# Linear attention: GpSimd's first split behind the second norm, and the next layer's first weights and chunk prepared in the last batch

## The chip, the cores and the metric

The kernel runs on one core of a Trainium2 chip. A core has five engines with queues of their own: PE (TensorE, matmuls), DVE (VectorE), ACT (ScalarE), POOL (GpSimd) and SP (SyncE, which here only issues transfers). Engines wait for each other through semaphores. The metric is the device time of one execution in microseconds (us), the median of three runs.

## What is computed

Two transformer layers over 4 batches of 1024 tokens with 512 features. The change touches the second layer: a linear attention, and the feed-forward network behind it. The reference, cut to these:

```python
# linear attention (16 heads of 32; x is the normalized output of layer 0)
Q = jax.nn.relu(x @ Wq.T + bq); K = jax.nn.relu(x @ Wk.T + bk); V = x @ Wv.T + bv
Q = Q * decay; K = K * decay                       # exp(-pos / n)
KV = jnp.einsum('bhnd,bhne->bhde', K, V); Ksum = K.sum(axis=2)
Z = 1.0 / (jnp.einsum('bhnd,bhd->bhn', Q, Ksum)[..., None] + EPS)
out = jnp.einsum('bhnd,bhde->bhne', Q, KV) * Z
x = layernorm(x + out @ Wo.T + bo)
# feed-forward
X = x.reshape(-1, H).astype(jnp.float16)
D = gelu(X.astype(jnp.float32) @ W0.T + bias0).astype(jnp.float16)
E = D.astype(jnp.float32) @ W1.T + bias1
x = layernorm(x + E.astype(jnp.float16))
```

Wherever a product of 32-bit values has to keep its accuracy, both sides are split into a high part (rounded to the matmul's 32-bit format, "fp32r") and a low part (value minus high part), and the products of the parts are summed.

## The kernel before

The program is a row of phases; each allocates its buffers and semaphores, runs one block in which every engine has its own queue of instructions, and ends with a barrier of all engines. A semaphore that starts above zero is incremented by GpSimd at the start of its phase, in the order in which the code allocates them (line 63).

**Linear attention (`phase_linear_attention`, 503 us).** It works in chunks of 512 tokens, two a batch. Vector takes layer 0's output `y` in three passes (`quantize`, L1931 to L1935), adds the residual (`add_x1`, L1944) and normalizes (`LayerNorm`: four statistics L1206, aggregates L1210, on GpSimd an add and the power -0.5 in `pool_part`, L1193 and L1195, then on Vector four normalizing passes L1216). TensorE transposes the chunk (L1834); ScalarE copies the high part out of PSUM (L1798), Vector makes the low part (`part_lo`, L1951). TensorE then makes queries, keys and values (all matmuls of `partials` stand under L1164), four PSUM banks at a time. ScalarE finishes the queries (L1820), Vector adds the biases to keys (L1968) and values (L1974), GpSimd adds the output bias to the residual (L1772) and applies the decay (L1780, L1786). Then come the products of keys and values (taken by Vector at L1994), those with the queries (L1907), the division (L2011), transposes of the result, and the output projection, half by half, which Vector adds to the reloaded residual (L2024) and normalizes; SyncE stores each chunk to `x3_dram` (L1745). For batch b, Vector also prepares batch b+1. The work of all batches but the last stands in a hardware loop, that of the last behind it (`batches`).

The output weights `wo` are loaded into the buffer `ks`, which later holds the keys. ScalarE makes their high part and GpSimd their low part (`split_loader`, L99), two halves of 1024 columns. GpSimd does this between the first chunk's `pool_part` and the second's:

```python
ln_a.pool_part(pool, 0)
split_lo(pool)
ln_a.pool_part(pool, 1)
```

The phase ends when the last chunks are stored and landed and the first chunk of `x3` has been loaded for the next phase.

**Last layer (`phase_ffn1`, 498 us).** GpSimd builds a 16-bit identity (L2122, L2124). Vector casts chunk 0 to 16 bit (L2235), TensorE transposes it (L2179), ScalarE copies it to `xT` (L2152). Then, for each of 16 hidden tiles of each of 8 chunks: eight matmuls into a bank (`hidden`), gelu on ScalarE (L2165), a cast on GpSimd (L2141), eight matmuls into four output banks (`to_y`, L2205). TensorE is one hidden tile ahead. Both weights are loaded and split on Vector (L2242, L2244) from the start of the phase on, in 16 blocks of 1024 columns in turn; TensorE waits for the blocks in order.

## Time and profile before

| what | value |
|---|---|
| median of three runs | 2501.93 us (2501.62 to 2502.35) |
| the profiled execution's own time | 2500.06 us |
| its span | 2498.4 us |
| mean granted clock of TensorE | 0.983 of full |
| TensorE busy | 2377.2 us, 95% |
| VectorE, ScalarE, GpSimd busy | 1210.2, 817.8, 867.4 us |
| the chain that ended last | PE 19%, all other engines 0% |

The profile is of one execution. Its span runs from the first to the last instruction; its own time adds what lies around it. TensorE is busy nearly always, so a microsecond of another engine counts only where TensorE then waits. A busy TensorE need not be a fast one: its granted clock is 1.0 (2.4 GHz) or 0.5 (1.2 GHz).

### The profile page before, as it was taken

Reading aid. Unit: us, or ns where it says so; the run is one execution under the profiler, and the core shown is the slowest. Engines: PE = TensorE matmul, PEld = TensorE weight load, DVE = VectorE, ACT = ScalarE, POOL = GpSimd, SP = SyncE. Lnnn points to the kernel's source line nnn. Section 1 sums busy time; section 2 is a strip of 40 time slices with the busy share of each in tenths; the row PEclk is TensorE's granted clock in tenths of the full one; section 3 lists DMA queues with packets and bytes.
Section 4 is the critical chain, followed back from the end, with each engine's and each line's share of the span. In section 5 each row is a group of like instructions: output and inputs, shape, how many; then the busy total and the mean of one; then the engine's idle time right before and its main releaser. Section 6 shows DMA issues by size and latency. Waiting matters only on the chain. (4 is left out here: it accounts for less than half of the span.)

```text
span 2498.4 us, 39792 instructions
## 1 busy us (share of the span) xinstructions
PE 2377.2 (95%) x12757; PEld 1781.4 (71%) x12757; DVE 1210.2 (48%) x2540; ACT 817.8 (33%) x1387; POOL 867.4 (35%) x1097
## 2 busy tenths in 40 slices
PE   7999899999999999899999985999999799999997
PEld 5888655555555558688888874888888678888886
DVE  3334477777777758322222217676863551112211
ACT  3222255555555544344444431111111022222221
POOL 2000065565665642233333335242515022222221
PEclk9999999999999999999999997999999999999999
DMA  6885344545445337412121104040311250000100
GB/s 236 285 292 201 114 112 118 131 116 134 114 118 138 91 118 270 118 35 51 34 50 34 51 32 159 17 168 34 134 50 51 85 156 34 34 34 34 36 32 34
DMA packets 210065, 255.16 MB, mean 102 GB/s; under 512 B 68931, under 2 KB 106819, under 8 KB 209989
## 3 DMA queue, kind: packets, MB, share of 16 engines
q1 hardware_dynamic: 194084, 210.04, 28.5%
...
## 5 line engine op out<-in xcount | busy, mean ns | idle before, releaser
L177 DVE CUSTOM_DVE_ANT_0 junk<-psum,causal 128x896 bf16<-128x896 f32 (+7 forms) x512 | 373.6, 751 | 169.3 <-PE psum L887 145.0
L996 ACT ACTIVATE p_probs<-psum 128x512 f32<-128x512 f32 (+1 forms) x640 | 317.9, 555 | 274.9 <-PE psum L900 270.0
L1499 POOL TENSOR_TENSOR p_h_lo<-p_h,p_h_hi 128x512 fp32r<-128x512 f32 x128 | 164.3, 1284 | 307.9 <-ACT p_h_hi L1524 307.9
L900 PE MATMUL psum<-qst,kst 98*128 98x512 f32 (+3 forms) x768 | 223.6, 370 | 6.4 <-POOL p_ones L739 5.9
L2141 POOL CAST p_h<-p_h 128x512 fp32r<-128x512 f16 x128 | 92.0, 719 | 372.9 <-ACT p_h L2165 372.9
L789 POOL TENSOR_SCALAR_AFFINE_SELECT p_probs<-p_probs 128x128 f32<-128x128 f32 x512 | 141.5, 298 | 227.7 <-ACT p_probs L996 224.5
L900 PEld LDWEIGHTS psum<-qst,kst 98*128 98x128 f32 x768 | 132.3, 191 | 111.8 <-DVE rowmax L177 42.6
L887 PE MATMUL psum<-kst,qst 96*128 96x128 f32 (+3 forms) x720 | 208.1, 364 | 0.0
L1164 PE MATMUL psum<-p_xT,p_w_hi 128*128 128x512 f32 x512 | 203.2, 397 | 0.7 <-ACT p_xT L2152 0.7
L1553 PE MATMUL psum<-tern,p_h_hi 128*128 128x512 f32 x512 | 199.4, 390 | 2.0 <-POOL p_h_lo L1499 2.0
L1164 PE MATMUL psum<-p_xT,p_w_lo 128*128 128x512 f32 x512 | 200.2, 391 | 0.0
L2205 PE MATMUL psum<-p_w_hi,p_h 128*128 128x512 f32 x512 | 199.4, 389 | 0.3 <-POOL p_h L2141 0.3
L1553 PE MATMUL psum<-tern,p_h_lo 128*128 128x512 f32 x512 | 199.2, 389 | 0.0
L2205 PE MATMUL psum<-p_w_lo,p_h 128*128 128x512 f32 x512 | 199.2, 389 | 0.0
L2165 ACT ACTIVATE p_h<-psum,p_b 128x512 f16<-128x512 f32 x128 | 88.0, 687 | 330.6 <-PE psum L1164 330.6
L1516 ACT ACTIVATE p_h<-psum,ffn_b,alpha 128x512 f32<-128x512 f32 x128 | 99.8, 780 | 260.3 <-PE psum L1164 260.3
L887 PEld LDWEIGHTS psum<-kst,qst 96*128 96x128 f32 x720 | 125.3, 191 | 67.8 <-DVE rowmax L177 41.1
L2254 DVE TENSOR_TENSOR p_e<-psum,p_b 128x512 f16<-128x512 f32 x32 | 19.9, 682 | 299.9 <-PE psum L2205 299.9
L916 PE MATMUL psum<-p_probs,v 128*32 128x512 f32 (+3 forms) x1536 | 157.9, 498 | 1.8 <-ACT p_probs L996 1.1
L927 PE MATMUL psum<-p_probs,p_ones 128*32 128x512 f32 (+3 forms) x1536 | 154.8, 490 | 0.0
L403 PE MATMUL psum<-p_xT_hi,p_w_hi 128*128 128x512 f32 x256 | 100.8, 394 | 17.5 <-DVE p_w_lo L99 17.5
L1553 PEld LDWEIGHTS psum<-tern,p_h_hi 128*128 128x128 f32 x512 | 96.1, 188 | 22.7 <-POOL p_h_lo L1499 1.5
...
## 6 DMA issues: line engine op xcount, KB each, us to landing
...
```

Of the source, the lines that this page charges most:

```text
L177: return dve.tensor_tensor_reduce(view(junk[:, 0:n]), bank, view(self.causal[:, SEQ - n:SEQ]), 1.0, FLOOR, ALU.add, ALU.max, self.rowmax[: ...
L403: mm = pe.matmul(bank, lhsT, rhs, start=(n == 0), stop=(n == 3 * KT - 1))
L789: pool.affine_select(out=blk, in_=blk, compare_op=ALU.is_ge, fill=0.0, base=0, pattern=[[1, P]], channel_multiplier=-1).then_inc(p_masked, 1)
L887: mm = pe.matmul(psum[:, bank, 0:keys], qst[slot][0:KD, c, g, tile * P:(tile + 1) * P], kst[slot][0:KD, g, k0:k0 + keys], start=True, stop ...
L900: mm = pe.matmul(psum[:, bank, col:col + CH - q0], kst[s][0:KD + 2, g, j * P:(j + 1) * P], qst[s][0:KD + 2, c, g, q0:CH], start=True, stop ...
L916: mm = pe.matmul(O_BANK[g * HD:(g + 1) * HD, q0:CH], vs[s][:, j, g * HD:(g + 1) * HD], probs[:, n % 2, g, col:col + CH - q0], start=(n == ...
L927: mm = pe.matmul(SUM_BANK[g * HD:(g + 1) * HD, q0:CH], ones[:, :], probs[:, n % 2, g, col:col + CH - q0], start=(n == half_at), stop=(n + ...
L996: act.activation(probs[:, n % 2, g, col:CH], psum[:, banks_of(s, "s", st)[0], col:CH], ACT.Exp, scale=SM_SCALE).then_inc(p_ready, 1)
L1164: mm = pe.matmul(bank, lhsT, rhs, start=(n == 0), stop=(n == len(terms) - 1))
L1499: pool.tensor_tensor(h_lo[:, m % 2, :], h[:, m % 2, :], f32(h_hi[:, m % 2, :]), ALU.subtract).then_inc(hl_done, 1)
L1553: mm = pe.matmul(Y.bank(m), src[:, t % 2, tok], tern2[:, t, :], start=(t == 0 and part == 0), stop=(t == HT - 1 and part == 1))
L2205: mm = pe.matmul(Y.bank(m), h[:, t % 2, a * P:(a + 1) * P], w[:, t, :], start=(t == 0 and part == 0), stop=(t == HT - 1 and part == 1))
```

## The change

1. GpSimd does both chunks' `pool_part` first, waits for the second norm (`ln_a.normed`), and only then splits `wo`. Vector waits for this split before it writes its first keys, and no longer before its loop. The semaphores `y_loaded` and `x1_loaded` are allocated first in the phase.
2. In the last batch SyncE loads, as buffers come free, the four row tiles of `W0` (2048 columns each), the first four of the 16 tiles of `W1`, chunks 0 and 1 of `x3`, and the bias. ScalarE makes the five high parts behind the last queries, Vector the low parts in three groups: two between keys and values of the second half, one behind the values, two behind the low parts of the output. The order is tile 3 of `W0`, then `W1`'s, then tiles 0, 1, 2. The buffers are those of weights, `y` and residual that are then free.
3. In the last batch Vector casts chunk 0 to 16 bit; TensorE transposes it between the two halves of the output projection, ScalarE copies it to `xT` and loads the gelu table; behind the output projection TensorE makes hidden tile 0 of the last layer. GpSimd builds the identity at the start of the linear attention.
4. In the last batch each statistic follows its add. SyncE no longer waits at the end of the phase for the stores of `x3`; SyncE and Vector wait for them in the last layer, before they use them.
5. The last layer starts with hidden tile 1, and splits only the twelve other tiles of `W1`. The PSUM banks of hidden tiles, transposes and outputs are 0 and 1, 2 and 3, 4 to 7.

The diff, cut to its core:

```diff
@@ -1202,8 +1202,15 @@
     def find_statistics(self, dve, n, src):
 
         for t in range(CT):
-            dve.wait_ge(self.summed, self.FROM + n * CT + t + 1)
-            dve.bn_stats(self.stats[:, t, :], src(t)).then_inc(self.got_stats, 1)
+            self.statistics_of(dve, n, t, src)
+        self.aggregate(dve, n)
+
+    def statistics_of(self, dve, n, t, src):
+        dve.wait_ge(self.summed, self.FROM + n * CT + t + 1)
+        dve.bn_stats(self.stats[:, t, :], src(t)).then_inc(self.got_stats, 1)
+
+    def aggregate(self, dve, n):
+
...
@@ class LastLayer @@
+    FIRST = 4
+
+    def hidden(self, pe, bank, c, t):
+        return partials(pe, bank, [(w[k][:, t * P:(t + 1) * P], self.xT[:, c, k, :]) for k in range(KT) for w in (self.w0_hi, self.w0_lo)])
...
+        y_loaded = [sem("p5_y_loaded0", 16), sem("p5_y_loaded1")]
+        x1_loaded = sem("p5_x1_loaded", 16)
         wo_hi = sb("p5_wo_hi", [P, KT, D], F32R)
...
-        y_loaded = [sem("p5_y_loaded0", 16), sem("p5_y_loaded1")]
-        x1_loaded = sem("p5_x1_loaded", 16)
...
+        parts = [(after.w0_raw[k], after.w0_hi[k], after.w0_lo[k]) for k in (3, 0, 1, 2)]
+        parts.insert(1, (after.w1_raw, after.w1_hi, after.w1_lo))
...
@@ -1727,26 +1773,48 @@
                 sp.wait_ge(ln_a.summed, ln_a.FROM + CT)
                 load_x1(sp, 0, 1)
 
+                def load_tile(n, k):
+                    sp.dma_start(after.w0_raw[k], after.w0[k * P:(k + 1) * P, :]).then_inc(raw_loaded[n], 16)
+
+                def load_next(b):
+
+                    sp.wait_ge(ln_a.summed, ln_a.FROM + 8 * b + 8)
+                    load_tile(0, 3)
+                    for c in range(2):
+                        sp.wait_ge(x3_stored[c], 1 + 16)
+                        sp.dma_start(by_tile(after.x3[c]), tiles(x3_dram[c])).then_inc(next_loaded, 16)
+                    sp.dma_start(after.b0c, after.b0).then_inc(b0_loaded, 16)
+
+                def load_weights(b):
+
+                    for c in range(2):
+                        sp.wait_ge(residual_stored[c], 16 * b + 16)
+                    sp.wait_ge(t_lo, 1 + 16 * b + 8)
+                    sp.dma_start(after.w1_raw, after.w1[0:after.FIRST * P, :].rearrange("(t p) n -> p t n", p=P)).then_inc(raw_loaded[1], 16)
+                    for k, freed in enumerate((q_relu, k_biased, v_done)):
+                        sp.wait_ge(freed, 8 * b + 8)
+                        load_tile(2 + k, k)
+
                 def body(b, last):
+                    if last:
+                        load_next(b)
                     for c in range(2):
                         sp.wait_ge(x2_biased, 2 * b + c + 1)
                         sp.dma_start(tiles(residual[2 * b + c]), chunk(x2, c)).then_inc(residual_stored[c], 16)
+                    if last:
+                        load_weights(b)
                     for c in range(2):
                         sp.wait_ge(residual_stored[c], 16 * b + 16)
                         sp.sem_inc(passed, 1)
                         sp.wait_ge(t_lo, 1 + 16 * b + 8 + 4 * c + 4)
                         sp.sem_inc(passed, 1)
                         sp.dma_start(chunk(ks, c), tiles(residual[2 * b + c])).then_inc(residual_loaded[c], 16)
-                    if last:
-                        sp.wait_ge(x3_stored[0], 1 + 16 * b)
-                        sp.dma_start(by_tile(next_x3[:, :]), tiles(x3_dram[0])).then_inc(next_loaded, 16)
                     for c in range(2):
                         sp.wait_ge(ln_b.normed, 8 * b + 4 * c + 4)
                         sp.dma_start(tiles(x3_dram[2 * b + c]), chunk(ks, c)).then_inc(x3_stored[c], 16)
                 batches(sp, body)
-                for c in range(2):
-                    sp.wait_ge(x3_stored[c], 1 + 16 * BATCH)
-                sp.wait_ge(next_loaded, 16)
+                sp.wait_ge(next_loaded, 32)
+                sp.wait_ge(b0_loaded, 16)
...
+                build(11, pool.memset(ident16[:, :], 0.0))
+                build(12, pool.affine_select(out=ident16[:, :], in_=ident16[:, :], compare_op=ALU.not_equal, fill=1.0, base=0,
+                                             pattern=[[-1, P]], channel_multiplier=1))
                 ln_a.setup(pool)
                 ln_b.setup(pool)
-                ln_a.pool_part(pool, 0)
+                for c in range(2):
+                    ln_a.pool_part(pool, c)
+                pool.wait_ge(ln_a.normed, 2 * CT)
                 split_lo(pool)
-                ln_a.pool_part(pool, 1)
...
@@ -1808,6 +1880,12 @@
                         for c in range(2):
                             load_y(act, b + 1, c)
                         load_x1(act, b + 1, 0)
+                    def next_hi():
+                        for n in range(KT + 1):
+                            act.wait_ge(raw_loaded[n], 16)
+                            raw, hi, _ = [flat(part) for part in parts[n]]
+                            act.activation(hi, raw, ACT.Copy).then_inc(raw_hi, 1)
+
                     for c in range(2):
                         if c == 1:
                             part_hi(b, 1, a_x)
@@ -1818,10 +1896,17 @@
                             m = b_q(c, g)
                             B.wait_full(act, b, m)
                             act.activation(qT[:, g, c * CH:(c + 1) * CH], B.bank(m), ACT.Relu, bias=bq_c[:, g:g + 1]).then_inc(q_relu, 1)
+                    if last:
+                        next_hi()
                     for c in range(2):
                         part_hi(b, c, a_oT)
                     if not last:
                         part_hi(b + 1, 0, a_x)
+                    else:
+                        for k in range(KT):
+                            A.wait_full(act, b + 1, k)
+                            act.activation(aT_hi[:, 0, k, :], A.bank(k).bitcast(F16)[:, 0:CH], ACT.Copy).then_inc(x_ready, 1)
+                        act.preload_act_table(ACT.Gelu)
...
@@ -1918,6 +2003,18 @@
                             B.fill(partials(pe, B.bank(m), product(c, 3, tok(t), everything, True)), m)
                         if c == 0 and not last:
                             x2_transposes(b + 1, 0)
+                        if c == 0 and last:
+                            pe.wait_ge(built, 12)
+                            pe.wait_ge(x_cast, 1)
+                            for k in range(KT):
+                                free_a(b + 1, k)
+                                for t in range(CT):
+                                    mm = pe.transpose(A.bank(k).bitcast(F16)[:, tok(t)], x16[:, t, tok(k)], ident16[:, :])
+                                A.fill(mm, k)
+                    if last:
+                        pe.wait_ge(x_ready, KT)
+                        pe.wait_ge(raw_lo, KT + 1)
+                        after.hidden(pe, psum[:, 0, :], 0, 0)
...
                 def body(b, last):
                     def keys(c):
+                        if c == 0:
+                            dve.wait_ge(w_done, n_w)
                         dve.wait_ge(x3_stored[c], 1 + 16 * b)
                         for t in range(CT):
                             B.wait_full(dve, b, b_k(c, t))
@@ -1974,6 +2072,12 @@
                             dve.tensor_tensor(vs[:, CT * c + t, :, 0:P], heads(B.bank(b_v(c, t))), heads(bias[:, 1, :]), ALU.add).then_inc(v_done, 1)
 
 
+                    def next_lo(first, to):
+                        for n in range(first, to):
+                            dve.wait_ge(raw_hi, n + 1)
+                            raw, hi, lo = [flat(part) for part in parts[n]]
+                            dve.tensor_tensor(lo, raw, f32(hi), ALU.subtract).then_inc(raw_lo, 1)
+
                     if not last:
                         quantize(b + 1, 0)
                     part_lo(b, 1, a_x, 0)
@@ -1981,7 +2085,14 @@
                         keys(c)
                         if not last:
                             add_x1(b + 1, c)
+                        if last and c == 1:
+                            next_lo(0, 2)
                         values(c)
+                        if last and c == 1:
+                            next_lo(2, 3)
+                            dve.wait_ge(next_loaded, 32)
+                            dve.wait_ge(q_done, 8 * b + 8)
+                            dve.tensor_copy(flat(x16), after.x3[0]).then_inc(x_cast, 1)
                         if not last:
                             ln_a.find_statistics(dve, 2 * b + 2 + c, x2_tile(c))
                         if c == 0 and not last:
@@ -2013,17 +2124,24 @@
                             ins.then_inc(o_done, 1)
                     for c in range(2):
                         part_lo(b, c, a_oT, 8)
+                    if last:
+                        next_lo(3, 5)
                     if not last:
                         ln_a.normalize_tiles(dve, 2 * b + 3, x2_tile(1), x2_tile(1))
                     for c in range(2):
                         dve.wait_ge(residual_loaded[c], 16 * b + 16)
+                        x3_tile = lambda t: ks[:, CT * c + t, :]
                         for t in range(CT):
                             m = b_out(CT * c + t)
-                            at = ks[:, CT * c + t, :]
                             B.wait_full(dve, b, m)
-                            dve.tensor_tensor(at, B.bank(m), at, ALU.add).then_inc(ln_b.summed, 1)
-                        x3_tile = lambda t: ks[:, CT * c + t, :]
-                        ln_b.vector_part(dve, 2 * b + c, x3_tile, x3_tile)
+                            dve.tensor_tensor(x3_tile(t), B.bank(m), x3_tile(t), ALU.add).then_inc(ln_b.summed, 1)
+                            if last:
+                                ln_b.statistics_of(dve, 2 * b + c, t, x3_tile)
+                        if last:
+                            ln_b.aggregate(dve, 2 * b + c)
+                        else:
+                            ln_b.find_statistics(dve, 2 * b + c, x3_tile)
+                        ln_b.normalize_tiles(dve, 2 * b + c, x3_tile, x3_tile)
 ...
@@ phase_ffn1 @@
+        H = Banks(nc, ctx, "p6_hbank", psum, 0, 2, 2 * HT, before=1)
+        h_done, h_used = sem("p6_h_done", 2), sem("p6_h_used", 1)
+        Y = Banks(nc, ctx, "p6_ybank", psum, 4, CT, 2 * CT)
+
+        T = Banks(nc, ctx, "p6_tbank", psum, 2, 2, 2 * KT)
+        bias_loaded = sem("p6_bias_loaded")
+        x_loaded = [sem(f"p6_x_loaded{c}", 16) for c in range(2)]
...
                sp.dma_start(b1r[:, :], rows(b1)).then_inc(bias_loaded, 16)
-                load_x(0, 1)
+                for c in range(2):
+                    sp.wait_ge(got.x3_stored[c], 1 + 16 * BATCH)
```

**How the order of instructions changes.** GpSimd, start of the linear attention, behind its memsets (`p_wo_lo` is the low part of `wo`, `p_k` and `ffn_rows` the buffer `ks`; x2 means two in a row). Before:

```order
L1186 MEMSET p_ln_a_power 128x4
L1186 MEMSET p_ln_b_power 128x4
L1193 TENSOR_SCALAR p_ln_a_vareps<-p_ln_a_meanvar 128x4
L1195 TENSOR_TENSOR p_ln_a_rstd<-p_ln_a_vareps,p_ln_a_power 128x4
L99 TENSOR_TENSOR p_wo_lo<-p_k,p_wo_hi 128x1024 x2
L1193 TENSOR_SCALAR p_ln_a_vareps<-p_ln_a_meanvar 128x4
L1195 TENSOR_TENSOR p_ln_a_rstd<-p_ln_a_vareps,p_ln_a_power 128x4
L106 UNCONDITIONAL_BRANCH
L106 ISA
L1772 TENSOR_TENSOR p_x<-p_x,p_bias 128x2048
```

With the change:

```order
L1829 MEMSET ident 128x128
L1830 AFFINE_SELECT ident<-ident 128x128
L1186 MEMSET p_ln_a_power 128x4
L1186 MEMSET p_ln_b_power 128x4
L1193 TENSOR_SCALAR p_ln_a_vareps<-p_ln_a_meanvar 128x4
L1195 TENSOR_TENSOR p_ln_a_rstd<-p_ln_a_vareps,p_ln_a_power 128x4
L1193 TENSOR_SCALAR p_ln_a_vareps<-p_ln_a_meanvar 128x4
L1195 TENSOR_TENSOR p_ln_a_rstd<-p_ln_a_vareps,p_ln_a_power 128x4
L99 TENSOR_TENSOR p_wo_lo<-ffn_rows,p_wo_hi 128x1024 x2
L106 UNCONDITIONAL_BRANCH
L106 ISA
L1844 TENSOR_TENSOR la_x<-la_x,p_bias 128x2048
```

The second root has moved ahead of the split, and the identity has been added ahead of both norms.

Vector, last batch, keys and values (`ffn_w_first` is the part of `W1`, `la_w_lo` takes tiles of `W0`, `p_decay_row` then holds the 16-bit chunk). With the change:

```order
L2048 TENSOR_TENSOR p_aT_lo<-psum,ffn_xT 128x512 x4
L2066 TENSOR_TENSOR ffn_rows<-psum,p_bias 128x512 x4
L2072 TENSOR_TENSOR p_v<-psum,p_bias 128x4x128 x4
L2066 TENSOR_TENSOR ffn_rows<-psum,p_bias 128x512 x4
L2079 TENSOR_TENSOR ffn_w_3<-la_y,ffn_w_3 128x2048
L2079 TENSOR_TENSOR ffn_w_first<-la_x,ffn_w_first 128x2048
L2072 TENSOR_TENSOR p_v<-psum,p_bias 128x4x128 x4
L2079 TENSOR_TENSOR la_w_lo<-ffn_w_raw,la_w_hi 128x2048
L2095 CAST p_decay_row<-ffn_x 128x2048
L2105 TENSOR_TENSOR p_kv<-psum,p_same_head 128x128
L2106 TENSOR_SCALAR p_kv<-p_same_head,psum 128x4
```

The rows with 128x2048 are new: two subtractions ahead of the second half's values, one subtraction and the cast behind them; two more stand behind the low parts of the output.

TensorE, end of the linear attention and start of the last layer. Before:

```order
L1164 MATMUL psum<-p_wo_lo,p_aT_hi 128x512
L1716 UNCONDITIONAL_BRANCH
L2170 UNCONDITIONAL_BRANCH
L2179 MATMUL psum<-p_ident,p_x 128x128 x16
L1164 MATMUL psum<-p_xT,p_w_hi 128x512
L1164 MATMUL psum<-p_xT,p_w_lo 128x512
L1164 MATMUL psum<-p_xT,p_w_hi 128x512
L1164 MATMUL psum<-p_xT,p_w_lo 128x512
```

With the change:

```order
L1164 MATMUL psum<-p_wo_hi,p_aT_lo 128x512
L1164 MATMUL psum<-p_wo_lo,ffn_xT 128x512
L1164 MATMUL psum<-ffn_xT,la_w_hi 128x512
L1164 MATMUL psum<-ffn_xT,la_w_lo 128x512
L1164 MATMUL psum<-ffn_xT,la_w_hi 128x512
L1164 MATMUL psum<-ffn_xT,la_w_lo 128x512
L1164 MATMUL psum<-ffn_xT,la_w_hi 128x512
L1164 MATMUL psum<-ffn_xT,la_w_lo 128x512
L1164 MATMUL psum<-ffn_xT,ffn_w_3 128x512 x2
L1762 UNCONDITIONAL_BRANCH
L2257 UNCONDITIONAL_BRANCH
L106 UNCONDITIONAL_BRANCH
```

The 16 transposes have moved ahead of the second half of the output projection, and the eight matmuls of hidden tile 0 ahead of the phase's end.

## Rows read from the trace of the kernel before

**Rows 1.** Waits of TensorE over the whole span: us in total, times, longest.

```profile
PE psum L1834 <- DVE p_x L1216: 28.3, 2, 15.7
PE psum L2179 <- POOL p_ident L2124: 15.9, 1, 15.9
```

**Rows 2.** Timeline, linear attention, chunk 1: start, us, engine, line, operation.

```profile
1517.03 1.27 DVE L1931 TENSOR_SCALAR la_y<-la_y,la_quant 128x2048 f32<-128x2048 f32 x1
1517.30 6.59 POOL L99 TENSOR_TENSOR p_wo_lo<-p_k,p_wo_hi 128x1024 fp32r<-128x1024 f32 x2 [6.97 <-ACT p_wo_hi L94]
1518.34 3.31 DVE L1933 TENSOR_SCALAR la_y<-la_y 128x2048 f32<-128x2048 f32 x1
...
1525.01 2.50 DVE L1944 TENSOR_TENSOR p_x<-la_y,la_x 128x512 f32<-128x512 f32 x4
1527.70 0.94 ACTq L1711 DMA_DIRECT2D la_y<-ffn_out  x2
1531.94 4.49 POOL L1772 TENSOR_TENSOR p_x<-p_x,p_bias 128x2048 f32<-128x2048 f32 x1
1532.00 8.92 DVE L1216 TENSOR_SCALAR p_x<-p_x,p_ln_a_meanvar,p_ln_a_rstd 128x512 f32<-128x512 f32 x4 [1.58 <-POOL p_ln_a_rstd L1195]
1541.06 3.67 PE L1834 MATMUL psum<-ident,p_x 128*128 128x128 f32 x16 [12.61 <-DVE p_x L1216]
...
1550.78 0.69 DVE L1968 TENSOR_TENSOR p_k<-psum,p_bias 128x512 f32<-128x512 f32 x1 [2.03 <-PE psum L1164]
...
DMA to landing us min/median/max: 5.7/6.7/7.8
```

**Rows 3.** Timeline, start of the linear attention.

```profile
1499.49 1.29 DVE L1931 TENSOR_SCALAR la_y<-la_y,la_quant 128x2048 f32<-128x2048 f32 x1 [2.16 <-POOLq L63]
1499.87 1.05 POOL L1756 MEMSET p_same_head<- 128x132 f32 x1 [10.27 <-issue]
...
1503.39 2.50 DVE L1944 TENSOR_TENSOR p_x<-la_y,la_x 128x512 f32<-128x512 f32 x4
```

**Rows 4.** Timeline, end of the linear attention and start of the last layer.

```profile
1983.94 11.26 SPq L1745 DMA_DIRECT2D x<-p_k  x2
1988.29 2.46 DVE L1206 BATCH_NORM_STATS2 p_ln_b_stats<-p_k 128x6 f32<-128x512 f32 x4
1992.87 1.92 DVE L1216 TENSOR_SCALAR p_k<-p_k,p_ln_b_meanvar,p_ln_b_rstd 128x512 f32<-128x512 f32 x4 [1.58 <-POOL p_ln_b_rstd L1195]
...
2003.55 1.04 PE L2179 MATMUL psum<-p_ident,p_x 128*128 128x128 f16 x8 [15.90 <-POOL p_ident L2124]
...
2012.46 0.49 PE L2205 MATMUL psum<-p_w_hi,p_h 128*128 128x512 f32 x1 [0.30 <-POOL p_h L2141]
```

**Rows 5.** Stretches: us, TensorE busy (instructions), granted clock, DMA share, GB/s.

```profile
1026.00:1027.00 1.00, 1.00 (x4) 0.53 0.67 116
...
1544.00:1546.00 2.00, 2.00 (x8) 0.56 0.00 0
```

**Rows 6.** Groups by line and form, and the timeline of the last batch.

```profile
L1320 ACT ACTIVATE p_o_hi<-pieces 128x2048 fp32r<-128x2048 f32 x3 | 5.8, 1919 | 15.2 <-PE psum L1164 11.8 <-PE psum L1344 3.4
L1372 DVE TENSOR_TENSOR p_o_lo<-pieces,p_o_hi 128x2048 fp32r<-128x2048 f32 x3 | 6.8, 2258 | 0.0
...
1945.26 0.29 DVE L1994 TENSOR_TENSOR p_kv<-psum,p_same_head 128x128 f32<-128x128 f32 x1 [2.16 <-PE psum L1164]
...
1961.81 1.09 ACT L1798 ACTIVATE p_aT_hi<-psum 128x512 fp32r<-128x512 f32 x2 [40.47 <-PE psum L1834]
...
1970.71 1.35 DVE L2024 TENSOR_TENSOR p_k<-psum,p_k 128x512 f32<-128x512 f32 x2 [3.18 <-DMA p_k<-residual]
```

**Rows 7.** Timeline, start of layer 0's feed-forward phase.

```profile
1020.10 0.39 SPq L1286 DMA_DIRECT2D x<-p_x  x1
...
1022.66 0.79 PE L1164 MATMUL psum<-ffn_xT_hi,tern 128*128 128x512 f32 x1 [5.59 <-POOLq L63]
```

153 lines of the change are left out of this document (75 added, 78 removed).

## Prediction, made before the change was measured

> **What bounds the kernel now.** The waits of TensorE come first, because TensorE is busy for 95% of the span: only its idle time can be taken away, or its work. Two of the waits lie in the phases that the change touches: 28.3 us in two waits for the first norm's output of the linear attention's first two chunks, and 15.9 us for the 16-bit identity at the start of the last layer [rows 1]. I then read the timelines around both places, engine by engine, for the chain that ends each wait, and last the clock.
>
> *Place A, start of the linear attention.* TensorE has chunk 0's queries, is through at 1528.45 and waits 12.61 us, until 1541.06 [rows 2]. Vector makes that wait: three quantizing passes over chunk 1 last from 1517.03 to 1525.01, 7.98 us, where the same three over chunk 0 last 3.90 (1499.49 to 1503.39) [rows 2, 3]. Add, statistics and the reciprocal root lead to 1532.00, and the four normalizing passes then take 8.92 us, where four such passes alone take 1.92 [rows 2, 4]. Both slow stretches lie beside GpSimd work: the split of the output weights (6.59 us) and the bias add (4.49 us) [rows 2].
>
> *Place B, end of the linear attention and start of the last layer.* The last statistics start at 1988.29, SyncE has issued the last store at 1995.20, and the first output matmul of the last layer is at 2012.46. Between them lie the store's landing, the barrier, the identity, 16 transposes and two hidden tiles, the first of them at half clock [rows 4].
>
> **The change, part by part.**
>
> *1. Start values.* GpSimd increments 21 semaphores when the phase begins. The one that Vector's first pass waits for was the 17th and is now the first. GpSimd's own first instruction starts 0.38 us after Vector's, with four increments between: 0.095 us each [rows 3]. Sixteen fewer would be 1.5 us; nothing is the other end, if the barrier is what lasts. I take 1.0, nearer to the increments, since Vector's wait ends on GpSimd's queue by the row itself. The added 16-bit memset and select lie between 1499.87 and the first root, which can't be asked for before four adds (2.50) and four statistics are through; with a memset at 1.05 they fit, and cost nothing [rows 3, 4].
>
> *2. GpSimd's split behind the second norm.* Vector's chunk 1 then runs without GpSimd's big operations: 7.98 becomes 3.90 and 8.92 becomes 1.92, together 11.08 us. With part 1 the norm ends 12.08 us earlier, and the transposes start at 1528.98. TensorE's own queue ends 1.0 earlier too, at 1527.45, so 12.61 us of idling become 1.5. In the kernel before the clock stood at its lower level (0.5, 1.2 GHz) from 1541.06 until about 1545.76 [rows 2, 5]; 4.7 us at half speed are 2.35 us of work lost. An idle time of 1.5 us is far shorter than the one after which it was low, so I give back all of that. **Place A gives 14.4 us.**
>
> What is late next is GpSimd: its split and first bias add, and what Vector does beside them. The next values' bank needs key tile 0, one projection (four banks of 2.72) after the key projection starts: 1528.98 + 1.84 (16 transposes, half of the 3.67 that they take at the low clock) + 10.88 = 1541.7. Vector has by then to quantize batch 1's first chunk beside GpSimd (7.98, as chunk 1 before), make four low parts and one key tile, all five 512 wide from PSUM at the key tile's 0.69: 1528.84 + 7.98 + 3.45 = 1540.3 [rows 2]. The slack is 1.4 us, and it depends on who goes first. In the rows, a single-input Vector pass that starts at 1518.34 lasts 3.31 instead of about 1.25: it starts while GpSimd's operation runs and ends 1.1 after that one must be through, so the two take turns by whole instructions.
>
> The Trainium skill, "SBUF — State Buffer", section on the two sides of SBUF, says the same in general: the pair of ports that VectorE and GpSimd share is an exclusive lock, held by whoever starts first for the whole instruction. By that rule GpSimd first means that Vector's third pass waits for the bias add as a whole, and the sum loses the 3.0 us of rival 2; by a shared bandwidth it would lose nothing. The trace agrees with the lock.
>
> *3. Weights in the last batch.* Five tiles of 2048 columns are loaded, copied on ScalarE (1.92 each) and subtracted on Vector (2.26 each) [rows 6]. ScalarE: the last load starts when the last value tile is biased (1943.1, that is 1945.26 less its idle 2.16), lands 5.7 to 7.8 later [rows 2, 6], and is copied by 1952.8 at the latest; ScalarE is next needed at 1961.81. Slack 9.0. Vector, behind the keys: two subtractions, 4.5 us, delay two or three value tiles, not the last, since TensorE makes one per 2.72. Behind the values: one subtraction and the 16-bit cast (at most 1.3, as a single-input pass), 3.6 us from 1943.1, so the first of the four key-value products is taken 1.4 late, and each later one comes as it did. Behind the low parts, from 1967.53 (1970.71 less 3.18): two subtractions until 1972.05, so the first residual add is 1.3 us late; add and statistics take 1.3 of every 2.72, and the delay is gone by the fourth tile. Cover gone in each case: up to 1.4. SyncE's queue now holds 3 MB ahead of the residual store; only two loads wait for that store, that of the second weights and, much later in the program, the residual's own, and both have room. All of it: zero.
>
> *4. The transition.* TensorE gets 16 transposes of 16 bit between the two halves of the output projection. Eight of them take 1.04 us at the low clock [rows 4], so 16 take 1.05 to 1.7 (as 32-bit ones); I take 1.3. The last chunk's chain starts that much later: 1989.59 for its first statistic. Three of four statistics now lie between the adds (2.46 / 4 each, 1.85 off): the last store is issued by 1989.59 + 6.91 - 1.85 = 1994.65. Its landing is no longer waited for. At the other phase start where TensorE had its operands ready, it began 2.17 us after the last store was issued (1020.49 to 1022.66), behind 14 increments [rows 7]; now it needs four of them. Ends 1.0 and 2.17, taken 1.3: hidden tile 1 starts at 1995.95. Hidden tile 0 has been made before the barrier, and its gelu and cast run beside tile 1. The clock: TensorE idles about 5 us, and in two rows it took 4.2 and 4.7 us of matmuls until the clock was up again [rows 2, 5, 7]; I take low from the start for 4.5 us, 2.25 lost (ends: never low, 0; 6.4 us as at 2003.55, 3.2). Hidden tile 1 is 8 matmuls, 1.81 at full clock (2.72 / 12 each). At full speed the first output matmul would thus stand at 1995.95 + 1.81 + 2.25 = 2000.0, against 2012.46. **Place B gives 12.45 us.** The twelve tiles of the second weights that are still split after the barrier are needed only from the fifth step on.
>
> *Sum.* 14.4 + 12.45 = 26.85. The profiled execution took 2500.06, so 2473.2; the median of the runs shown is 1.87 above that execution, so **2475.1**. Everything after place A and place B is TensorE without waits, so both shifts last to the end.
>
> **The rivals.**
> 1. *My sum, within its bounds:* from 2472.3 (clock never low, 0.5 more at place A) to 2478.4. Chance 0.5.
> 2. *GpSimd gets the ports first at place A.* Then its two halves of the split (4.49 / 2 = 2.25 each) and the bias add alternate with Vector's passes (1.1 each): 1531.2, 1532.3, 1534.55, 1535.65, 1540.1, 1541.2; low parts and key tile end at 1544.65, and TensorE waits 3.0 us. It decides by batch 1's first y: issued at 1522.6, 5.7 to 7.8 until landing, 1528.3 or later, against 1528.84 when Vector is free [rows 2]. Time 2478.1. For: 0.5 us of margin. Against: the first of two loads is the quicker. Chance 0.23.
> 3. *The last batch or the transition does only a part.* Either the phase's end still waits for the store (what lies between 1995.20 and 2003.55, less 2.17: up to 6.2; 2479 to 2481), or the delays of part 3 reach TensorE, each up to 1.4 and more if a load is late. Time 2479 to 2485. Chance 0.24.
> 4. *Slower than before.* ScalarE takes the five weight tiles in order ahead of the copies of the attention's transposed output. If the last load is late by more than 9.0 us, each further microsecond holds TensorE; slower than before from 36 us late on (9.0 + 26.85), 2502 and more. No load in the rows takes over 7.8. Chance 0.01; 0.02 remain for no difference.
>
> **How the numbers follow.** A run of this kernel can be told from another one by about 0.2%, 5 us; all cases but the last two are faster by more. The predicted time is that of case 1. The range takes in case 1, case 2 with its own late end (2481), and most of case 3: 2470.5 to 2484. Faster 0.97, same 0.02, slower 0.01.
>
> **What would show it.** TensorE's wait for the norm in one piece of about 15 us and one under 2; Vector's chunk 1 passes at 1.3 us, its normalizing at 1.92; the split of the output weights beside batch 1's quantizing; no more than 1 us of waiting before the first values (3 would be rival 2). At the end: 16 transposes between the output halves; a gap of about 5 us from hidden tile 0 to tile 1; tile 1 at half clock. Wrong would be: a wait of TensorE for low parts, keys or weights in the last batch, a gap over 8 us at the transition, or steps of the last layer longer than before.

## The result, and the profile after

The changed kernel takes 2477.77 us (median of 4 runs, 2477.44 to 2478.64). The kernel before, timed on the same chip in the same sitting, takes 2502.14 us (4 runs, 2501.62 to 2502.47). The ratio is 0.9903, with a 95% interval of 0.9886 to 0.9920: faster, by 24.4 us. The forecast was 2475.1, with a range of 2470.5 to 2484.

The page of the changed kernel, parts of its head and its busy times:

```profile
span 2475.2 us, 39666 instructions
PE 2376.8 (96%) x12757; PEld 1779.9 (72%) x12757; DVE 1197.2 (48%) x2525; ACT 827.1 (33%) x1392; POOL 867.7 (35%) x1097
```

TensorE's busy time is what it was (2377.2 before); the span is shorter by 23.2 us, and 22.8 us of that are idle time of TensorE (121.2 us before, 98.4 now). Its mean granted clock went from 0.983 to 0.987. The waits of TensorE (total, times, longest) that answer to [rows 1]:

```profile
PE psum L1919 <- DVE la_x L1223: 16.3, 2, 14.8
PE psum L1164 <- POOLq L63: 11.4, 2, 5.8
PE psum L1164 <- DVE p_v L2072: 4.4, 4, 1.5
```

The wait for the norm's output has gone from 28.3 us in two pieces to 16.3, of which 14.8 is the first chunk's. The 15.9 us for the 16-bit identity are gone. In their place the second line, which was 5.6 us in one piece, has a second piece of 5.8 us: the gap at the barrier. The wait for the values, 2.9 us before, has grown to 4.4, by one piece of 1.5: that one is new, and the forecast did not have it.

**Place A.** Start of the linear attention, timeline of the changed kernel: start, duration, engine, line, operation, instructions, idle time before it. It answers to [rows 2, 3]. (All of this execution is already 0.30 us later than the one before when the phase begins.)

```profile
1498.75 1.29 DVE L2028 TENSOR_SCALAR la_y<-la_y,la_quant 128x2048 f32<-128x2048 f32 x1 [1.12 <-POOLq L63]
1516.67 1.28 DVE L2028 TENSOR_SCALAR la_y<-la_y,la_quant 128x2048 f32<-128x2048 f32 x1
1527.56 1.92 DVE L1223 TENSOR_SCALAR la_x<-la_x,p_ln_a_meanvar,p_ln_a_rstd 128x512 f32<-128x512 f32 x4 [1.58 <-POOL p_ln_a_rstd L1195]
1529.39 1.28 DVE L2028 TENSOR_SCALAR la_y<-la_y,la_quant 128x2048 f32<-128x2048 f32 x1
1529.56 6.70 POOL L99 TENSOR_TENSOR p_wo_lo<-ffn_rows,p_wo_hi 128x1024 fp32r<-128x1024 f32 x2 [2.03 <-DVE la_x L1223]
1529.61 1.97 PE L1919 MATMUL psum<-ident,la_x 128*128 128x128 f32 x16 [1.53 <-DVE la_x L1223]
1530.71 3.30 DVE L2030 TENSOR_SCALAR la_y<-la_y 128x2048 f32<-128x2048 f32 x1
1536.22 5.62 POOL L1844 TENSOR_TENSOR la_x<-la_x,p_bias 128x2048 f32<-128x2048 f32 x1
1542.33 0.41 SPq L1803 DMA_DIRECT2D residual<-la_x  x1
1546.77 7.33 DVE L2041 TENSOR_TENSOR la_x<-la_y,la_x 128x512 f32<-128x512 f32 x4 [3.54 <-DMA residual<-la_x]
1546.81 5.13 POOL L1844 TENSOR_TENSOR la_x<-la_x,p_bias 128x2048 f32<-128x2048 f32 x1
1554.03 2.47 DVE L2072 TENSOR_TENSOR p_v<-psum,p_bias 128x512 f32<-128x512 f32 x4
1554.85 0.47 PE L1164 MATMUL psum<-ffn_xT,la_w_hi 128*128 128x512 f32 x1 [1.48 <-DVE p_v L2072]
1557.86 0.69 ACT L1898 ACTIVATE p_qT<-psum,p_bq 128x512 f32<-128x512 f32 x1 [25.50 <-PE psum L1164]
1560.58 0.69 ACT L1898 ACTIVATE p_qT<-psum,p_bq 128x512 f32<-128x512 f32 x1 [2.03 <-PE psum L1164]
```

The first pass starts 1.12 us after what came ahead, not 2.16. Chunk 1's first pass takes 1.28 and the normalizing 1.92, as alone. The transposes run at once, and in 1.97 us instead of 3.67. Behind them GpSimd's split (6.70 us) lies beside batch 1's quantizing, whose second and third passes take 3.30 and 3.29. New is what follows: four residual adds take 7.33 us, not 2.50, beside GpSimd's second bias add; the first value is copied only at 1554.03, and TensorE waits.

**The last batch.** Timeline of the weight work that was moved there:

```profile
1920.19 2.28 DVE L2079 TENSOR_TENSOR ffn_w<-la_y,ffn_w 128x2048 fp32r<-128x2048 f32 x1
1920.48 5.98 POOL L1858 TENSOR_SCALAR ffn_rows<-ffn_rows,p_decay_col 128x512 f32<-128x512 f32 x1 [0.72 <-DVE ffn_rows L2066]
1922.39 2.29 DVE L2079 TENSOR_TENSOR ffn_w_first<-la_x,ffn_w_first 128x2048 fp32r<-128x2048 f32 x1
```

Each subtraction takes 2.25 to 2.3 us, as forecast from [rows 6]. Beside two of them one of GpSimd's key decays takes 5.98 us; the three ahead of it take 2.00. No wait of TensorE came of any of it.

**Place B.** The transition to the last layer, timeline, answering to [rows 4]:

```profile
1977.50 0.69 DVE L1210 BATCH_NORM_STATS2 p_ln_b_stats<-ffn_rows 128x6 f32<-128x512 f32 x1
1982.26 0.38 SPq L1814 DMA_DIRECT2D x<-ffn_rows  x1
1984.36 0.79 PE L1164 MATMUL psum<-ffn_xT,la_w_hi 128*128 128x512 f32 x1 [5.81 <-POOLq L63]
1984.36 0.69 ACT L2252 ACTIVATE p_h<-psum,ffn_b 128x512 f16<-128x512 f32 x1 [15.87 <-POOLq L63]
1992.76 0.69 ACT L2252 ACTIVATE p_h<-psum,ffn_b 128x512 f16<-128x512 f32 x1 [3.82 <-PE psum L1164]
```

Windows of the same stretch (us, busy time of TensorE, its weight loads, VectorE, ScalarE and GpSimd, then granted clock, share of the DMA engines, GB/s):

```profile
1982.00:1983.00 1.00, 0.00 (x0) 0.00 (x0) 0.24 (x1) 0.00 (x0) 0.00 (x0) 0.99 0.00 0
1983.00:1984.00 1.00, 0.00 (x0) 0.00 (x0) 0.00 (x0) 0.00 (x0) 0.00 (x0) 0.50 0.81 309
1989.00:1990.00 1.00, 1.00 (x4) 0.76 (x4) 0.83 (x2) 0.00 (x0) 0.73 (x1) 0.60 1.06 397
```

SyncE's last store is issued at 1982.26 and TensorE goes on at 1984.36; hidden tile 1 and more run at half clock until about 1989.7. For the accounts below, the same two anchors in the kernel before, the first query tile of chunk 1 and the third gelu of the last layer:

```profile
1569.82 0.69 ACT L1820 ACTIVATE p_qT<-psum,p_bq 128x512 f32<-128x512 f32 x1 [24.46 <-PE psum L1164]
2016.49 0.69 ACT L2165 ACTIVATE p_h<-psum,p_b 128x512 f16<-128x512 f32 x1 [3.53 <-PE psum L1164]
```

### The profile page after: what moved, and what is told of

It reads as the page before. It is cut to its first block and busy times, and to the rows that moved or that the text cites. A ratio compares the mean times of both kernels' runs of the same rounds, so it can differ in the third digit from the quotient of the medians.

```text
span 2475.2 us, 39666 instructions
## 1 busy us (share of the span) xinstructions
PE 2376.8 (96%) x12757; PEld 1779.9 (72%) x12757; DVE 1197.2 (48%) x2525; ACT 827.1 (33%) x1392; POOL 867.7 (35%) x1097
## 5 line engine op out<-in xcount | busy, mean ns | idle before, releaser
L1164 PE MATMUL psum<-ffn_xT,la_w_hi 128*128 128x512 f32 x512 | 202.9, 396 | 8.8 <-POOLq L63 5.8
L2252 ACT ACTIVATE p_h<-psum,ffn_b 128x512 f16<-128x512 f32 x128 | 88.0, 688 | 346.6 <-PE psum L1164 330.7
L1164 PE MATMUL psum<-ffn_xT,la_w_lo 128*128 128x512 f32 x512 | 200.5, 392 | 0.0
L2336 DVE TENSOR_TENSOR ffn_rows<-psum,p_b 128x512 f16<-128x512 f32 x32 | 19.9, 684 | 315.7 <-PE psum L2286 315.7
L2286 PE MATMUL psum<-p_w_hi,p_h 128*128 128x512 f32 x384 | 149.7, 390 | 0.0
L2286 PE MATMUL psum<-p_w_lo,p_h 128*128 128x512 f32 x384 | 149.5, 389 | 0.0
L1164 PEld LDWEIGHTS psum<-ffn_xT,la_w_hi 128*128 128x128 f32 x512 | 96.6, 189 | 29.3 <-POOLq L63 6.2
```

Of the source, the lines that this page charges most:

```text
L1164: mm = pe.matmul(bank, lhsT, rhs, start=(n == 0), stop=(n == len(terms) - 1))
L2286: mm = pe.matmul(Y.bank(m), h[:, t % 2, a * P:(a + 1) * P], w(t), start=(t == 0 and part == 0), stop=(t == HT - 1 and part == 1))
```

## The experiments

The kernel before was timed again beside each group of runs; its medians were 2501.02, 2501.71 and 2502.07 us, and 2502.14 above. So medians of different groups can differ by about 1 us for nothing. Where an effect is smaller, the timeline within the run decides, and the text says which of the two it goes by.

### Is it GpSimd's place that made chunk 1 slow?

Run *split_between* puts the split back between the two roots. With it goes GpSimd's wait for the second norm (`ln_a.normed`), which in the changed kernel keeps the bias add and the query decay off that norm as well:

```diff
-for c in range(2):
-    ln_a.pool_part(pool, c)
-pool.wait_ge(ln_a.normed, 2 * CT)
-split_lo(pool)
+ln_a.pool_part(pool, 0)
+split_lo(pool)
+ln_a.pool_part(pool, 1)
```

> The changed kernel with one part undone: GpSimd's split of the output weights stands between its two first reciprocal roots again; everything else stays. Theory (Vector's chunk 1 was slow because GpSimd's big operations lay beside it): the three quantizing passes take about 8 us again in place of 3.8, the norm behind them about 8.9 in place of 1.92, TensorE waits over 12 us before chunk 1's transposes and comes out of it at its lower clock, and the 1.48 us wait before the first values is gone. That is 12 to 13 us back: 2489.5 to 2491. Rival (chunk 1 was slow from its own load or from the late start): the passes stay near 1.3 us and the time within 2 us of 2477.8.

Measured: 2487.92 us (2487.53 to 2489.06), 10.2 more than the changed kernel; ratio to before 0.9948 (0.9931 to 0.9964), against 0.9903, which is 11.2 us.

```profile
1517.42 3.30 DVE L2029 TENSOR_SCALAR la_y<-la_y 128x2048 f32<-128x2048 f32 x1
1531.08 8.92 DVE L1223 TENSOR_SCALAR la_x<-la_x,p_ln_a_meanvar,p_ln_a_rstd 128x512 f32<-128x512 f32 x4 [1.58 <-POOL p_ln_a_rstd L1195]
1540.13 3.67 PE L1918 MATMUL psum<-ident,la_x 128*128 128x128 f32 x16 [12.64 <-DVE la_x L1223]
```

The second pass takes 3.30 us again (so does the third), the norm's four passes take 8.92, and TensorE waits 12.6 us for them. The slow passes lie beside the split and cost 4.08 us; the slow norm lies beside the bias add (from 1531.02, 4.49 us) and the query decay behind it, and costs 7.00. The run undoes both at once, so it shows that GpSimd's order made the 11 us; how they divide is read from the timeline, and no run has the one without the other. The wait before the first values is gone (2.9 us in all). The first query tile of chunk 1 stands at 1569.43, 11.57 later than in the changed kernel, and this run began the phase 0.45 earlier: 12.0 us, as the theory says. The medians lie 1.6 under the lower end of my range. 0.7 of that is the clock at the transition, which came back sooner in this run (first to third gelu 7.67 us, against 8.40); the rest is no more than groups of runs differ by.

*start_alone* is the kernel before with place A's parts alone (the order above; the three load semaphores allocated first; Vector's wait for the split of the output weights moved down):

```diff
+y_loaded = [sem("p5_y_loaded0", 16), sem("p5_y_loaded1")]
+x1_loaded = sem("p5_x1_loaded", 16)
...
-dve.wait_ge(w_done, n_w)
...
 def keys(c):
+    if c == 0:
+        dve.wait_ge(w_done, n_w)
```

> The kernel before with only the parts at the start of the linear attention: the split behind the second root, the three load semaphores ahead of the others, Vector's wait for the weights' load behind the quantizing passes. Nothing in the last batch or the transition. Theory (the two places add up, nothing is shared): the whole of place A and nothing of place B, 12 us off, 2489.5 to 2490.5, with Vector's passes as in the changed kernel. Rival (part of place B's gain comes from place A, or the other way round): outside 2488 to 2492.

Measured: 2489.64 us (2489.22 to 2491.28), 11.4 less than before in the same group; ratio 0.9956 (0.9939 to 0.9972). The first query tile of chunk 1 stands at 1558.06 there, against 1569.82 in the kernel before and 1557.86 in the changed one. This run began the phase 0.23 us later than the changed kernel, so place A is worth the same with and without place B, 12.3 us at that point. By the medians it is 11.4, and 11.9 more for all else in the changed kernel (their sum of 23.3 misses 24.4 by the 1.1 by which the kernel before differs between the two groups). Place B alone was not run.

### Part 1: the start values

*semaphores_late* allocates `y_loaded` and `x1_loaded` of the changed kernel behind the 16 others again.

> The changed kernel with the load semaphores of the first pass back behind 16 others, so GpSimd increments their start values last. Theory (Vector's first pass waits for that increment): the first pass starts 1.0 us later after the phase before, and the time is 1.0 us more, 2478.8. Rival (the barrier or another engine lasts longer): no change, 2477.8.

Measured: 2477.67 us (2477.11 to 2477.94), by the median no change. The timeline of this run:

```profile
1499.80 1.29 DVE L2028 TENSOR_SCALAR la_y<-la_y,la_quant 128x2048 f32<-128x2048 f32 x1 [2.31 <-POOLq L63]
1558.97 0.69 ACT L1898 ACTIVATE p_qT<-psum,p_bq 128x512 f32<-128x512 f32 x1 [25.19 <-PE psum L1164]
```

Vector's first pass does wait 2.31 us in place of 1.12, and the first query tile comes 1.11 us later (1558.97 against 1557.86), though this run began the phase 0.14 us earlier. So the increments are what Vector waited for, and the move is worth 1.2 us there. At the other end of the program only 0.6 are left (span 2475.8 against 2475.2): at the transition this run's clock came back 0.5 us earlier after hidden tile 1 (first to third gelu 7.86 us, against 8.40). The theory holds for the place; end to end, it is inside what these runs can tell.

### The new wait: adds beside a bias add

Vector's four adds, one by one, in the changed kernel (first and second):

```profile
1546.77 0.69 DVE L2041 TENSOR_TENSOR la_x<-la_y,la_x 128x512 f32<-128x512 f32 x1 [3.54 <-DMA residual<-la_x]
1547.38 5.11 DVE L2041 TENSOR_TENSOR la_x<-la_y,la_x 128x512 f32<-128x512 f32 x1
```

The second lasts 5.11 us: it ends 0.55 us after GpSimd's bias add does (1546.81 + 5.13 = 1551.94). Two runs ask whether that is the cause. *no_second_bias* leaves GpSimd's second bias add out but for 8 columns:

```diff
-pool.tensor_tensor(part, part, bias..., ALU.add).then_inc(x2_biased, 1)
+if c == 0:
+    pool.tensor_tensor(part, part, bias..., ALU.add).then_inc(x2_biased, 1)
+else:
+    pool.tensor_tensor(part[:, 0:1, 0:8], part[:, 0:1, 0:8], bias[:, 2:3, 0:8], ALU.add).then_inc(x2_biased, 1)
```

> The changed kernel without most of GpSimd's second output-bias add of each batch (the output bias is missing from the second half of each batch, but for 8 columns). It asks what makes the new wait of 1.48 us before the first values, where Vector's four residual adds take 7.33 us and start beside GpSimd's second bias add of 5.13 us. Theory (Vector and GpSimd lock each other out of SBUF's shared ports): the adds take 2.5 us, TensorE's wait before the first values is gone, the time 1.5 us less, 2476.3, and a little more in the eight batches if something there was hidden. Rival (the residual's store and load make the chunk late): the wait stays at 1.0 us or more, 2477.3 or above.

Measured: 2476.34 us (2474.70 to 2477.35).

```profile
1546.73 2.92 DVE L2044 TENSOR_TENSOR la_x<-la_y,la_x 128x512 f32<-128x512 f32 x4 [3.57 <-DMA residual<-la_x]
1558.78 0.69 ACT L1901 ACTIVATE p_qT<-psum,p_bq 128x512 f32<-128x512 f32 x1 [2.03 <-PE psum L1164]
```

*values_first* keeps all the work and puts the first chunk's adds behind its values:

```diff
 keys(c)
-if not last:
+if not last and c == 1:
     add_x1(b + 1, c)
...
 values(c)
+if not last and c == 0:
+    add_x1(b + 1, c)
```

> The changed kernel with the residual add of each batch's first chunk behind that batch's first values instead of ahead of them. Theory (TensorE's wait of 1.48 us before the first values comes from the 7.33 us adds that stand ahead of the values in Vector's queue): the values' first copy starts as soon as TensorE has made the tile, the wait is gone, the first query tile is 1.5 us earlier, 2476.3. Rival (the adds were free there and now delay the low parts or a later norm): the wait is gone and another of 1 us or more stands at the next chunk's transposes, 2477.5 to 2480.

Measured: 2476.26 us (2474.81 to 2476.93).

```profile
1553.77 1.99 POOL L1858 TENSOR_SCALAR ffn_rows<-ffn_rows,p_decay_col 128x512 f32<-128x512 f32 x1
1554.36 2.49 DVE L2041 TENSOR_TENSOR la_x<-la_y,la_x 128x512 f32<-128x512 f32 x4
1555.74 2.89 POOL L1858 TENSOR_SCALAR ffn_rows<-ffn_rows,p_decay_col 128x512 f32<-128x512 f32 x1
1559.19 0.69 ACT L1898 ACTIVATE p_qT<-psum,p_bq 128x512 f32<-128x512 f32 x1 [1.13 <-PE psum L1164]
```

The adds take 2.9 and 2.5 us, and TensorE's waits for values are back at 2.9 us in all. In *values_first* ScalarE takes the first query tile late, since the issue of a load that waits for the adds stands ahead in its queue, so the second one is the anchor: 1560.58 in the changed kernel, 1558.78 without the bias add, 1559.19 with the values first (in a run 0.34 us later at chunk 1's norm), that is 1.8 and 1.7 us earlier. With *no_second_bias* the adds start when they did (1546.73), after the same wait for the residual's store, and TensorE waits for nothing more than in the kernel before; so that store alone does not make TensorE wait, and the rival falls. The store has a part in it all the same. Vector was through with its keys at 1543.2 and waited 3.54 us for it, and only therefore did the adds start beside the second bias add, which began at 1546.81. No other wait of TensorE grew in *values_first*, so its rival falls too. The medians are 1.4 and 1.5 us lower, in the direction and size of the theory, but within what groups of runs can differ; the lengths of the adds carry the verdict.

### Place B, piece by piece

*store_waited* lets SyncE wait for the last stores again at the end of the linear attention:

```diff
+for c in range(2):
+    sp.wait_ge(x3_stored[c], 1 + 16 * BATCH)
 sp.wait_ge(next_loaded, 32)
```

> The changed kernel with the wait for the last output stores at the end of the linear attention put back. Theory (the transition is shorter by the store's landing): the barrier opens 4 to 6 us later, TensorE's gap between hidden tiles 0 and 1 grows from 5.8 to 10 to 12 us, 2482 to 2484. Rival (the stores land while the last statistics are made, and the gain is in the early tile alone): the gap stays under 7 us, and the time within 1 us of 2477.8.

Measured: 2482.40 us (2481.66 to 2483.01).

```profile
1984.07 0.38 SPq L1814 DMA_DIRECT2D x<-ffn_rows  x1
1990.04 0.79 PE L1164 MATMUL psum<-ffn_xT,la_w_hi 128*128 128x512 f32 x1 [9.69 <-POOLq L63]
```

From the last store's issue to TensorE's next matmul it is 5.97 us here, and 2.10 in the changed kernel: 3.9 us is what the landing costs, 4.6 with the clock and the rest by the medians.

*tile_behind* makes hidden tile 0 in the last layer, behind the barrier:

```diff
 pe.wait_ge(raw_lo, KT + 1)
-after.hidden(pe, psum[:, 0, :], 0, 0)
...
-H = Banks(nc, ctx, "p6_hbank", psum, 0, 2, 2 * HT, before=1)
+H = Banks(nc, ctx, "p6_hbank", psum, 0, 2, 2 * HT)
...
+H.fill(got.hidden(pe, H.bank(0), 0, 0), 0)
```

> The changed kernel with hidden tile 0 of the last layer made behind the barrier, as the kernel before does, instead of ahead of it; transposes and the rest stay early. Theory (the tile's 8 matmuls fill waiting time ahead of the barrier, and behind it they are on the path at the lower clock): hidden tile 0 costs 3.6 us there, minus nothing, since the clock's fall lasts for 5 us either way; TensorE's gap is 1.8 us longer on its front side. 1.8 us of work more on the path, and the clock's loss unchanged: 2479.5 to 2481.5. Rival (TensorE would otherwise wait for the gelu and its cast before the first output matmul, so the tile's time is hidden behind them): under 1 us.

Measured: 2481.18 us (2481.09 to 2481.87), 3.4 more.

```profile
1983.48 0.38 SPq L1814 DMA_DIRECT2D x<-ffn_rows  x1
1986.66 0.77 PE L1164 MATMUL psum<-ffn_xT,la_w_hi 128*128 128x512 f32 x1 [8.71 <-POOLq L63]
```

The last store's issue to the first matmul is 3.18 us, against 2.10: TensorE waits 1.1 us longer behind the barrier, by the row for GpSimd's queue at the line of the start values. The code gives a reason: this run's hidden tile 0 first waits for the two banks of the transposes, whose start values come 14 increments behind the one that hidden tile 1 waits for. In *semaphores_late* 16 increments took 1.19 us, and at that rate 14 take 1.0. No run moves them here, so this is worked out and not shown. With the tile's 1.8 us that makes 2.9, which is also by how much the third gelu is later (1996.89, less 1.21 by which this run's last statistics are later, against 1992.76). I had the 1.8 and not the 1.1. The early tile is worth 3 us.

*statistics_together* puts the last batch's statistics behind all four adds of their chunk:

```diff
-if last:
-    ln_b.statistics_of(dve, 2 * b + c, t, x3_tile)
...
+ln_b.find_statistics(dve, 2 * b + c, x3_tile)
```

> The changed kernel with the last batch's statistics behind all four residual adds of a chunk again, as in the kernel before. Theory (they stand on the chain from the last output matmul to the barrier): last store and barrier 1.85 us later, 2479.6. Rival (TensorE's last products pace the adds, so the statistics between them cost what they save, or SyncE's queue is later anyway): under 0.5 us.

Measured: 2478.92 us (2478.15 to 2480.24), 1.2 more.

```profile
1986.66 0.79 PE L1164 MATMUL psum<-ffn_xT,la_w_hi 128*128 128x512 f32 x1 [7.42 <-POOLq L63]
```

The gap grows by 1.61 us, three of four statistics as forecast (1.85) less a little; 0.3 of it comes back as clock.

### The clock, at both places

*filler_end* keeps TensorE at work ahead of the barrier, with 16 matmuls into a bank that nobody reads:

```diff
 after.hidden(pe, psum[:, 0, :], 0, 0)
+for _ in range(2):
+    after.hidden(pe, psum[:, 1, :], 0, 0)
```

> The changed kernel with two more copies of the first hidden tile's 8 matmuls behind it, into a bank that nothing reads: 3.6 us of unused work in TensorE's gap of 5.8 us. Theory (hidden tile 1 runs at 1.2 GHz because of the gap ahead of it, and the gap is free time): the granted clock stays at 1.0 through the transition, the first gelus of the last layer are 3.7 us apart from the start in place of 3.9 and 4.5, and the time is 1.8 to 2.5 us less, 2475.3 to 2476. Rival (the fall comes from what remains of the gap, or the filler's end itself holds the barrier): the clock falls as before or the gap grows, 2477.5 to 2480.

Measured: 2475.65 us (2475.53 to 2476.40), 2.1 less.

```profile
1984.61 0.49 PE L1164 MATMUL psum<-ffn_xT,la_w_hi 128*128 128x512 f32 x1 [2.13 <-POOLq L63]
1987.34 0.95 PE L2288 MATMUL psum<-ffn_w_first,p_h 128*128 128x512 f32 x3 [0.63 <-POOL p_h L2234]
1991.36 0.69 ACT L2254 ACTIVATE p_h<-psum,ffn_b 128x512 f16<-128x512 f32 x1 [3.84 <-PE psum L1164]
```

```profile
1983.00:1984.00 1.00, 0.00 (x0) 0.00 (x0) 0.00 (x0) 0.00 (x0) 0.00 (x0) 1.00 0.53 203
```

The clock stays at 1.00 through the gap, now 2.13 us long, and the matmul behind it takes 0.49 us in place of 0.79. From the first to the third gelu it is 6.71 us, not 8.40: 1.7 us. It isn't more because TensorE, no longer slow, now waits 0.63 us for GpSimd's cast ahead of the first output matmul. This is the term of 2.25 to 2.7 us of my sum, tested by itself.

*filler_start* does the same ahead of the first norm of the linear attention, with 40 matmuls of 128x512:

```diff
+for n in range(10):
+    partials(pe, psum[:, 4 + n % 4, :], [(w_hi[n % 3][:, k, 0:P], w_hi[n % 3][:, k, :]) for k in range(KT)])
 x2_transposes(0, 0)
```

> The changed kernel with 40 unused matmuls of 128x512 ahead of chunk 0's transposes, in TensorE's wait of 14.8 us for the first norm at the start of the linear attention. Theory (the wait leaves TensorE at 1.2 GHz, its 16 transposes take 3.67 us in place of 1.97 and the low parts behind them come later): the granted clock is 1.0 when the norm is through, the transposes take 2 us, and the first query tile comes 1.7 to 2.0 us earlier, 2475.8 to 2476.1. Rival A (the transposes are paced by something else): the first query tile comes less than 0.5 us earlier. Rival B (chunk 1's norm is the later one, so what chunk 0 gains TensorE waits before chunk 1): TensorE's wait of 1.53 us before chunk 1's transposes grows by what chunk 0 gained, 2477.5.

Measured: 2476.13 us (2476.03 to 2476.53), 1.6 less by the median.

```profile
1498.28 10.88 PE L1164 MATMUL psum<-la_w_hi 128*128 128x512 f32 x40 [1.64 <-PEq L68]
1511.44 3.34 PE L1919 MATMUL psum<-ident,la_x 128*128 128x128 f32 x16 [2.27 <-DVE la_x L1223]
```

```profile
1511.00:1512.00 1.00, 0.56 (x4) 0.56 (x5) 0.39 (x1) 0.00 (x0) 0.00 (x0) 0.92 0.92 356
```

But the timeline doesn't show 1.6. The clock is up before the norm and falls at about 1511.8, with the transposes under way; these take 3.34 us where 1.97 was expected, and the low parts are paced by copies that take what they took. From the start of the norm to TensorE's first matmul behind it, it is 6.80 us (1509.47 to 1516.27), and 7.13 in the changed kernel (1509.75 to 1516.88): 0.33 us. Rival A's number came (less than 0.5 us), but not by its reason: the transposes were slow again since the clock fell, so the theory's own condition, a full clock for the transposes, wasn't met. The fall came 2.7 us after the last filler ended (1498.28 + 10.88 = 1509.16), though the transposes had begun by then (1511.44). Where the other microsecond of the median is from, these runs don't show.

*best* has *values_first*, *filler_end* and *filler_start* together.

> The changed kernel with the first chunk's residual add behind the first values, two unused hidden tiles in TensorE's gap at the transition, and 40 unused matmuls in its wait at the start of the linear attention. The first two have given 1.5 and 2.1 us alone, in different places. Theory (they add up, and the third gives up to 2 more): 2472.2 to 2474.2. Rival (the start's gain is taken by chunk 1's norm): 2474 to 2474.5. Either is faster than both kernels.

Measured: 2473.15 us (2473.01 to 2474.71); ratio to before 0.9887 (0.9871 to 0.9904). That is 28.9 us less than the kernel before in its group and 4.6 less than the changed kernel.

```profile
1558.15 0.69 ACT L1898 ACTIVATE p_qT<-psum,p_bq 128x512 f32<-128x512 f32 x1 [1.13 <-PE psum L1164]
1981.87 0.49 PE L1164 MATMUL psum<-ffn_xT,la_w_hi 128*128 128x512 f32 x1 [2.14 <-POOLq L63]
```

The gains stand where they stood alone: the second query tile is 2.4 us earlier than in the changed kernel (1558.15 against 1560.58), and the gap of 2.14 us passes with matmuls of 0.49 us behind it. The start gave more than in *filler_start*: the clock fell later among the transposes, at about 1512.4, they took 3.01 us, and from the norm to the first matmul it is 6.46 us, 0.67 less than in the changed kernel. The computation is the same; the 56 extra matmuls only fill idle time.

## Why the prediction was right, and where its terms were off

The direction, the places and most of the terms held. The sum was 26.85 us, against 24.4 by the medians and 23.2 by the two spans (the profiled execution of the kernel before was 2.1 us below its median, that of the changed one 0.2). The terms that were off erred in the same direction, so nothing cancelled there. But a part of the nearness is luck: the forecast of the profiled execution, 2473.2, missed its 2477.58 us by 4.4, and the forecast of the median missed by 2.7, since it added 1.87 us for a distance between the two that was 0.2 in the changed kernel.

*Start values.* Forecast 1.0, measured 1.04 (2.16 less 1.12). 0.38 of it was lost again: the adds took 2.61 instead of 2.50, and chunk 0's transposes 3.67 instead of 3.27, since they came earlier into the lower clock (it was up again at 1515.0 before and at 1515.3 after, and the transposes started at 1512.34 and 1511.72). The step "TensorE's own queue ends 1.0 earlier too" was off by that: it was 0.66.

*Quantizing and norm of chunk 1.* Forecast 11.08; the passes took 3.90 and 1.92 us, to the hundredth. *split_between* shows that GpSimd's order made the whole of it: by the timeline 4.08 us through the split's place, and 7.00 through the wait for the second norm, behind which the bias add and the query decay now come.

*The clock given back.* Forecast 2.35. From the transposes' start to the first query tile it was 28.76 us before (1541.06 to 1569.82), and is 28.25 (1529.61 to 1557.86) with a wait of 1.48 in it, so 26.77 without: 1.99 came back. Where the other 0.36 went was not taken apart.

*What is late next.* This is the step that failed. The prediction followed Vector up to the low parts and the key tile, asked who gets the ports first there (Vector, as forecast: rival 2 didn't come), and stopped. It had "the slack is 1.4 us", and no more than 1 us of waiting before the first values. The next piece of Vector's queue, four adds of two operands from SBUF, starts at 1546.77, 0.04 us ahead of the second bias add on GpSimd, and is held by it: 4.8 us longer, of which TensorE felt 1.48. GpSimd's work was not only moved behind the norm, it moved all that follows on its queue. The first bias add ended at 1541.84 and not at 1536.43, so the residual's store was issued only at 1542.33, and Vector's adds, which wait for it, came to stand beside the second bias add. That meeting had to be looked at in the same way as the one before the keys.

Place A therefore gave 14.4 - 0.34 - 0.36 - 1.48 = 12.2; by the anchor, 1569.82 - 1557.86 + 0.30 = 12.26.

The Trainium skill, "SBUF — State Buffer", section on the two sides of SBUF, names the second case too: a VectorE operation with two SBUF inputs and a GpSimd operation that reads SBUF exclude each other for the whole instruction. Here the second add ended 0.55 us after the bias add, and with the bias add gone the four took 2.92 us: these runs agree. *values_first* doesn't: there four such adds start while a key decay runs on GpSimd, and take their usual 2.49 us. The prediction had used that rule for the passes with one input only.

*Weights in the last batch.* Forecast zero, measured zero: no new wait of TensorE before the transition. GpSimd's key decay of 5.98 us was not in the working; nothing waited for it.

*The transition.* Forecast 12.45, measured 11.77 (2016.49 - 1992.76 = 23.73, plus 0.30, less 12.26). Two terms were too small: from the end of the last store's issue to TensorE 1.72 us, not 1.3 (within the ends of 1.0 and 2.17), and the lower clock lasted 5.4 us of matmuls, not 4.5, which costs 0.45 more; the two make 0.87, a little more than the 0.68 that is missing. The pieces by themselves: the stores' landing 3.9, the early tile 2.9, the statistics between the adds 1.2 to 1.6. No run takes out the rest by itself: the identity, the transposes and the weights made ahead.

*The last layer.* The prediction called longer steps a sign against it. 28 of them, all in groups of four, did last 3.97 us in place of 3.95, which makes 0.56 us, and leads from 23.73 to the 23.2 of the spans. No run asked why.

*The rivals.* Rival 3 (the phase's end waits for the store) didn't come; made on purpose it costs 4.6 us, within the "up to 6.2" given. Rival 4 had its loads on time.
